# Last expert mixture: expert rows added into a DRAM table by accumulating indirect DMAs, instead of gathered back

## The reference

```python
x = x + _L3_ffn_ref(_layernorm(x, axis=-1), L3_ffn_gate_w, L3_ffn_w1, L3_ffn_w2)

def _L3_ffn_ref(x, gate_w, w1, w2):
    router_logits = jnp.einsum('bsd,de->bse', x, gate_w)
    top_logits, top_idx = jax.lax.top_k(router_logits, TOP_K)
    top_w = jax.nn.softmax(top_logits, axis=-1)
    combine = jnp.sum(jax.nn.one_hot(top_idx, N_EXPERTS, dtype=x.dtype) * top_w[..., None], axis=-2)
    h = jax.nn.silu(jnp.einsum('bsd,edf->ebsf', x, w1))
    y = jnp.einsum('ebsf,efd->ebsd', h, w2)
    out = jnp.einsum('ebsd,bse->bsd', y, combine)
    return out
```

## Time and profile before

| | us |
|---|---|
| median of 3 runs (lowest to highest) | 2155.83 (2154.03 to 2156.53) |
| span of the profiled execution | 2156.2 |
| last sublayer: placement, 1916.25 (the store of `c_rows`) to 1940.24 (first gather) | 24.0 |
| loop, first gather to the end of the last copy to `y` (2105.14 + 0.37) | 165.3 |
| return, from there to the end of the span | 50.7 |

### The profile page before, as it was taken

One profiled execution on the slowest core, in us unless ns is written; L12 is line 12 of the kernel. 1 busy time (PEld: TensorE's weight loads), 2 busy tenths in 40 slices (PEclk: granted clock), 3 DMA queues, 4 the chain that ended last, 5 costly groups with the idle time before them and its releaser, 6 DMA issues. The chain is left out here.

```text
span 2156.2 us, 31922 instructions
## 1 busy us (share of the span) xinstructions
PE 1694.4 (79%) x9560; PEld 1268.2 (59%) x9561; DVE 1111.4 (52%) x2565; ACT 758.4 (35%) x1808; POOL 438.6 (20%) x451
## 2 busy tenths in 40 slices
PE   5965999999999999999997839629824479847990
PEld 4653666666666666666666629528713147636990
DVE  3335555556555655565554650157666856562212
ACT  1211544445444444444443213204426223312330
POOL 1012111111111221222211122241131500007005
PEclk9977999999999999999997559869957589958995
DMA  5001000000001000000000212151000000014114
GB/s 199 0 0 46 1 1 0 0 0 0 0 1 46 1 1 0 0 0 0 0 1 29 88 63 66 56 195 56 3 27 0 0 3 0 0 40 115 34 36 122
DMA packets 30065, 66.49 MB, mean 31 GB/s; under 512 B 6438, under 2 KB 21815, under 8 KB 28460
## 3 DMA queue, kind: packets, MB, share of 16 engines
q1 hardware_dynamic: 23900, 48.99, 6.3%
q0 software_dynamic: 6096, 16.65, 2.9%
HBM read 51.04 MB, written 14.59 MB: 30 GB/s over the span
## 5 line engine op out<-in xcount | busy, mean ns | idle before, releaser
L1052 PE MATMUL banks<-l_ffn_h2T,l_ffn_w 128*128 128x128 f32 (+1 forms) x1536 | 185.0, 279 | 32.2 <-ACT l_ffn_h2T L1166 32.2
L1052 PEld LDWEIGHTS banks<-l_ffn_h2T,l_ffn_w 128*128 128x128 f32 (+1 forms) x1536 | 173.8, 182 | 42.9 <-issue 39.0
L977 PE MATMUL banks<-l_ffn_in_wqkv,l_ffn_hT 128*128 128x512 f32 x384 | 197.2, 611 | 1.9 <-issue 1.1
L1146 ACT ACTIVATE l_ffn_work<-banks,l_ffn_att_bias,l_ffn_att_scale 128x256 f32<-128x256 f32 x256 | 140.6, 568 | 51.8 <-DVE l_ffn_att_bias L1287 51.8
L942 POOL TENSOR_TENSOR l_ffn_rstd<-l_ffn_ve,neg_half 128x1 f32<-128x1 f32 x32 | 17.8, 557 | 658.2 <-DVE l_ffn_ve L1315 658.2
L1015 PEld LDWEIGHTS banks<-l_ffn_vv,l_ffn_pT 128*128 128x128 f32 x1024 | 119.3, 195 | 33.3 <-ACT l_ffn_pT L1155 29.6
L999 PE MATMUL banks<-l_ffn_kT,l_ffn_qT 128*128 128x512 f32 x256 | 132.8, 601 | 0.0
L1015 PE MATMUL banks<-l_ffn_vv,l_ffn_pT 128*128 128x64 f32 x1024 | 122.7, 279 | 8.8 <-DVE l_ffn_pT L1293 5.1
L1286 DVE TENSOR_REDUCE l_ffn_att_top<-banks 128x2 f32<-128x512 f32 x128 | 88.5, 692 | 62.3 <-PE banks L999 62.3
L256 POOL TENSOR_TENSOR rstd<-mean_var,neg_half 128x1 f32 (+1 forms) x80 | 46.0, 576 | 346.9 <-DVE mean_var L249 346.7
L1176 ACT ACTIVATE l_ffn_gate<-banks,l_ffn_layer_cols 128x128 f32<-128x128 f32 x192 | 59.8, 362 | 136.5 <-PE banks L1052 136.5
(11 more groups left out here) (377 smaller groups left out, 3700.8 us busy)
## 6 DMA issues: line engine op xcount, KB each, us to landing
l_ffn_in_w<-in_L_w SPq DMA_DIRECT2D x2, 4096.0 KB, 20.2
l_experts_y_rows<-l_experts_y SPq DMA_DIRECT2D x63, 128.0 KB, 1.7
l_ffn_in_down<-in_L_down SPq DMA_DIRECT2D x1, 4096.0 KB, 13.0
l_experts_c_rows<-l_route_c_all SPq DMA_DIRECT2D x2, 2048.0 KB, 8.5
l_ffn_in_wqkv<-in_L_wqkv SPq DMA_DIRECT2D x1, 3072.0 KB, 12.8
l_ffn_w<-in_L_w SPq DMA_DIRECT2D x2, 1364.0 KB, 7.0
x_res<-in_x SPq DMA_DIRECT2D x4, 512.0 KB, 5.5
l_ffn_rot<-in_rotary SPq DMA_DIRECT2D x2, 1024.0 KB, 4.8
```

The lines of the kernel that those rows point to most:

```text
L977: mm = pe.matmul(ps[:, m.bank + 1 + n, :], hT[:, m.b, m.odd, ch, 1 - ch:P + 1 - ch], wqkv[:, bass.ds(m.layer, 1), ch, n * INNER:(n + 1) * ...
L1052: mm = pe.matmul(ps[0:FW[j], m.bank + j // 2, to:to + P], w1[:, ch, at:at + FW[j]], h2T[:, ch, m.b, :], start=(j % 2, n, ch) == (0, 0, 0), ...
L1146: ex = nc.scalar.activation(work[:, m.b, slot, :], ps[:, m.bank + slot // 2, (slot % 2) * 2 * P:(slot % 2 + 1) * 2 * P], ACT.Exp, bias=bia ...
```

## The change

`l3_ffn` calls a new function, `adding_experts`, in place of `experts`.

- `c_all` gets eight more columns, and `comb` is written into them, so a gathered row (264 wide) brings the token's eight weights with it. The DRAM table `c_rows` gets one more row, of zeros; empty slots take that row.
- `route` gets an SP block that stores `e.x` (2 MB) to the first 2048 rows of a new DRAM table `sums`, which has 128 rows more for empty slots.
- The placement computes, instead of `back` and the weights, which row of `sums` each slot belongs to (`to_row`). Its 32 products have 117 columns instead of 78, and seven small DVE steps follow them instead of two.
- In the loop ACT multiplies the product by the weight while it copies it: it loads the tile's expert number into a register and takes that column of the gathered rows as the scale. It waits for `y_added`, where it waited for SP's store of the same buffer.
- POOL issues 24 gathers, and then for each tile an indirect DMA that adds the 128 rows of `y` to rows of `sums` (line 2241 of the changed kernel). It issues one only when the one before has landed, since two tiles can hold the same token. The other 15 gathers come one behind each of the first 15 adds.
- The return gathers, the weighted sums on DVE and the eight output stores are gone. SP waits for all 39 adds and copies `sums` to the output by one DMA from DRAM to DRAM.

The diff, cut to what the steps above touch:

```diff
-    comb = sb("comb", every)
-    c_all = sb("c_all", [P, ALL_TILES, D])
+    c_all = sb("c_all", [P, ALL_TILES, D + wide])
+    comb = c_all[:, :, D:D + wide] if wide else sb("comb", every)
...
+        if x_to:
+            @block.sync
+            def _(sp):
+                sp.dma_start(x_to[0], e.x[:]).then_inc(x_to[1], 16)
...
+def adding_experts(e, ctx, stage, given, routed, n_tiles, up_weight, down_weight, sums, x_kept):
...
+        @block.gpsimd
+        def _(p):
+            def gather(t):
+                g = 0 if t < until[1] else 1 if t < until[2] else 2
+                p.indirect_dma_start(rows[:, t, :], None, c_rows, bass.IndirectOffsetOnAxis(ap=token[:, t:t + 1], axis=0))\
+                 .then_inc(gathered[g], 16)
+
+            p.wait_ge(c_kept, 32)
+            for t in range(until[2]):
+                gather(t)
+            p.wait_ge(x_kept, 16)
+            for t in range(n_tiles):
+                turn, j = divmod(t, WIDTH)
+                p.wait_ge(s.y_copied.sem, s.y_copied.at(turn, j + 1))
+                if t:
+                    p.wait_ge(added, 16 * t)
+                    p.sem_inc(s.y_added.sem, 1)
+                p.indirect_dma_start(sums, bass.IndirectOffsetOnAxis(ap=to_row[:, t:t + 1], axis=0), y[:, j, :], None, compute_op=ALU.add,
+                                     bounds_check=EMPTY + P - 1, oob_is_err=True).then_inc(added, 16)
+                if until[2] + t < n_tiles:
+                    gather(until[2] + t)
+            p.wait_ge(added, 16 * n_tiles)
+            p.sem_inc(s.y_added.sem, 1)
...
+            def copy_y(m):
+                act_.wait_ge(s.down_psum.sem, s.down_psum.at(m.turn, m.k))
+                act_.wait_ge(s.y_added.sem, s.y_added.at(m.turn, m.k - WIDTH))
+                x = act_.value_load(expert_of[0:1, bass.ds(m.turn * WIDTH + m.j, 1)], min_val=0, max_val=E8 - 1)
+                nc.scalar.activation(y[:, m.j, :], ps[3 + m.j][:, 0:D], ACT.Copy,
+                                     scale=flat(rows[:, bass.ds(m.turn * WIDTH + m.j, 1), bass.ds(x + D, 1)])).then_inc(s.y_copied.sem, 1)
...
+    with nc.Block() as block:
+        @block.sync
+        def _(sp):
+            sp.wait_ge(added, 16 * n_tiles)
+            sp.dma_start(e.out.rearrange("p k d -> (p k) d"), sums[0:EMPTY]).then_inc(e.stored, 16)
+            sp.wait_ge(e.stored, 16)
...
-        routed = route(e, ctx, "l3_route", given, False)
-        experts(e, ctx, "l3_experts", given, routed, KEEPING_TILES, False, lambda x: w1[:, bass.ds(x, 1), :, :].rearrange("p x c n -> p (x c n)"),
-                lambda x, f: w2[:, bass.ds(x, 1), f, :].rearrange("p x n -> p (x n)"), False)
+        x_to = sums[0:ALL_TILES * P].rearrange("(p k) d -> p k d", k=ALL_TILES)
+        routed = route(e, ctx, "l3_route", given, False, EXPERTS, (x_to, x_kept))
+        adding_experts(e, ctx, "l3_experts", given, routed, KEEPING_TILES, lambda x: w1[:, bass.ds(x, 1), :, :].rearrange("p x c n -> p (x c n)"),
+                       lambda x, f: w2[:, bass.ds(x, 1), f, :].rearrange("p x n -> p (x n)"), sums, x_kept)
```

More of the change, by code:

```diff
@@ L143, in __init__ @@
         self.y_copied = new("y_copied")
+        self.y_added = new("y_added")
         self.y_stored0 = new("y_stored0")
@@ L1600, in __init__, with route @@
                                     (self.p_col, "p_col"), (self.tri32, "tri")] + [(w, of) for w, (_, _, of) in zip(self.weights, weights)])
-def route(e, ctx, stage, given, gates_are_softmax):
+def route(e, ctx, stage, given, gates_are_softmax, wide=0, x_to=None):
     nc, s, ps = e.nc, e.s, e.ps
@@ L1665, in keep_c @@
                 k = m.it + m.b * TILES
-                v.tensor_scalar(tile_of(c_all, m.it, m.b), tile_of(e.x, m.it, m.b), flat(e.mean_var[:, bass.ds(k, 1), 0:1]),
+                v.tensor_scalar(tile_of(c_all[:, :, 0:D], m.it, m.b), tile_of(e.x, m.it, m.b), flat(e.mean_var[:, bass.ds(k, 1), 0:1]),
                                 e.rstd[:, bass.ds(k, 1)], ALU.subtract, ALU.mult)
@@ L2882, in l3_ffn @@
     w1, w2 = given.weights
+    sums = e.nc.dram_tensor("l3_sums", (ALL_TILES * P + P, D), F32).ap()
+    x_kept = e.dma_sem("l3_x_kept")
     with ExitStack() as ctx:
-        routed = route(e, ctx, "l3_route", given, False)
-        experts(e, ctx, "l3_experts", given, routed, KEEPING_TILES, False, lambda x: w1[:, bass.ds(x, 1), :, :].rearrange("p x c n -> p (x c n)"),
-                lambda x, f: w2[:, bass.ds(x, 1), f, :].rearrange("p x n -> p (x n)"), False)
+        x_to = sums[0:ALL_TILES * P].rearrange("(p k) d -> p k d", k=ALL_TILES)
+        routed = route(e, ctx, "l3_route", given, False, EXPERTS, (x_to, x_kept))
+        adding_experts(e, ctx, "l3_experts", given, routed, KEEPING_TILES, lambda x: w1[:, bass.ds(x, 1), :, :].rearrange("p x c n -> p (x c n)"),
+                       lambda x, f: w2[:, bass.ds(x, 1), f, :].rearrange("p x n -> p (x n)"), sums, x_kept)
 def rotary():
```

209 lines of the change are left out of this document (added).

## The result

| | us |
|---|---|
| predicted (8 in 10 range) | 2145 (2119 to 2190) |
| changed kernel, median of 4 runs | 2168.42 (2167.3 to 2173.03) |
| kernel before, median of 4 runs beside them | 2155.18 (2154.03 to 2156.53) |
| ratio, 95% interval | 1.0067 [1.0053, 1.0081] |
| span of the changed kernel's profiled execution | 2166.0 |

The change costs 13.2 us where 11 us less were forecast. This is the second rival, adds slower than break-even. A repeat on another chip gave 2166.45 us (9 runs), ratio 1.0041 [1.0027, 1.0055]; there the kernel before against itself came out at 0.9997 [0.9985, 1.0008].

What follows compares the result with a forecast made beforehand. PE was taken to bound the loop, with a 50.7 us return behind it. Terms: -50.7 return, +1.3 placement, +28.5 later end of adds, +9.9 rest: 11 us less than 2156.2, forecast 2145 us, range 2119 to 2190.

Steps and rivals of the forecast that it cites:

- the second rival: Chain of adds in the last loop: adds too slow, period up to 5.3 us, time 2160 to 2190 us; chance 0.33.
- break-even: Chain of adds: at a period of 4.48 us, 3.7 us to land, the span ends at 2156.2 as before.
- What bounds the kernel now: Last sublayer: PE paces the loop at 3.73 us a tile; the return behind it takes 50.7 us, all there is to win.
- Placement: Path to the first gather: wider products and seven small steps instead of two cost +1.3 us (bounds 0 and +2.2).
- ACT's register load: ACT's copy to `y` in the loop: a load of 0.58 us, hidden in 1.33 us free before silu.
- gathers between adds: POOL in the loop: gathers between the first 15 adds, 1.25 us each, fit into POOL's waiting and add nothing.
- clock: PE in the loop: busy 89%, its clock may fall to half, span 2267 us; held unlikely, chance 0.03.
- Value: 2.7 + 0.7 = 3.4, period T = 4.2 us: Each add: a gather's 2.7 us plus 0.7 for twice the bytes read, plus 0.8 wake-up; bounds 3.5 and 5.3.
- The chain as what decides: Loop: each add waits for the last one's landing, so 39 adds at 4.2 us pace it, ending at 2135.35.
- SP wakes 0.8 us later by the same step: End of the kernel: SP issues the output copy 0.8 us after the last add has landed.
- The rule of the Trainium skill: Price of an add: 2.6 us for 256 KB by this rule, so adds would keep up with PE; that rival's chance 0.12.
- The copy from DRAM to DRAM: End of the kernel: the 2 MB output copy takes 8.8 us, as the store of `c_rows` does (bounds 7 and 17.6).

Runs made afterwards that it cites:

- the scatter: The changed kernel with a plain indirect write in place of the accumulate, so table rows are overwritten: 2126.54 us (one run).
- the two tables: The changed kernel with odd tiles added to a second table, two adds in flight, both tables summed at the end: 2128.25 us, ratio 0.986 to the kernel before.
- chip 12: Repeat of the unaltered changed kernel beside the unaltered kernel before on another chip: 2166.45 against 2155.93 us.

## Why the prediction was wrong

- **What bounds the kernel now**: right. The return's 50.7 us went, the adds pace the loop, and 3.73 us for a tile was the right yardstick; the scatter and the two tables ran at 3.67 and 3.62.
- **Placement, ACT's register load, gathers between adds, clock**: right (1.2 us against 1.3; PE's pauses behind ACT 1.0 us at the most, and no loss of pace in the kernels whose adds do not hold ACT up; 1.80 us left over; clock 1.00).
- **"Value: 2.7 + 0.7 = 3.4, period T = 4.2 us"**: this term failed. It measured 3.8 and 4.67. The chain as what decides was right; the price of its link was off, and so was the reason for it. I priced the accumulation as twice the bytes read, +0.7 us over a gather. The plain scatter lands in 2.4, so the accumulation is +1.4, and in the place of more bytes the runs show 0.56 us of longer issue and three times the packets for the same bytes. Two errors partly cancel by luck: the gather's 2.7 was 0.3 above the operation's own base of 2.4, and the extra term 0.7 too small, so the landing is off by only 0.4. 39 x 0.4 of landing and 38 x 0.07 of wake are the 18.3 us. The forecast had named the condition: off by more than 0.3 us, it is wrong. I had also put POOL's longer issue among the reasons of the rival, with no price; it is 0.6 us for each add.
- **"SP wakes 0.8 us later by the same step"**: failed too, by 6.0 us. I took the wake of a store inside a block and overlooked that the copy stands in the next block, behind a barrier that drains POOL. The trace of before held such drains, one behind each of the two mixtures' loops, the second with 21.0 us:

```profile
L1893 POOLq DRAIN  x2: 18261/19636/21011, 1294.8 to 1974.5; - x2
```

  It was hidden because POOL had issued its last gather at 1989.4 and PE ran on until 2105. What ended last before was not POOL, so a drain cost nothing; now POOL ends last.
- **The copy from DRAM to DRAM**: right, 8.7 against 8.8.
- **The rule of the Trainium skill, "DMA: Bandwidth & Descriptors", section "Anatomy of one DMA"** (about 2.0 us fixed plus bytes by 436 GB/s): its estimate of 2.3 us for 128 KB agrees with the plain scatter's 2.4. For the add it gives 2.6 with twice the bytes, and the trace says 3.8; the measurement decides.
- **Break-even** was put at T = 4.48. With the measured tail it is 4.48 - 6.0 / 39 = 4.33; the measured 4.67 lies 0.34 above it, and 0.34 x 39 = 13.3 us agrees with the 13.2 measured. On chip 12, with a period of 4.63, it gives 11.9, and 9.9 were measured.

## What to carry to other kernels

A DMA that must wait for the one before it is priced by its full period, landing plus wake, and is to be held against the tile time of the engine it feeds; where it is longer, split the dependence (two tables) rather than shorten the operation. An accumulating indirect DMA is its own operation: take its time from one that accumulates. When POOL becomes the last engine of a block, its drain at the barrier comes onto the path, so issue the next DMA from inside the block. The other engines' drains at this barrier were short (ACT 0.36 us, DVE 0.55, PEld 1.38).

## What the runs showed of the hardware

- An indirect DMA of 128 rows of 1 KB that accumulates in DRAM: 1.55 us to issue on POOL and 3.8 to land; the same without accumulation 0.99 and 2.4; a gather 0.95 and 2.8 to 3.0 (medians of three lines), 2.6 at the least. With 512-byte rows the period of a chain is 4.27 instead of 4.60 to 4.69 us. Two in flight land in 4.0.
- The accumulating DMA has 144 packets for 0.13 MB, the plain scatter 48 for the same bytes.
- POOL's drain at the end of a block took 6.4 us from the landing of its last indirect DMA.
- A 2 MB copy from DRAM to DRAM landed in 8.2 to 8.8 us; a 2 MB store from SBUF in 6.3 (`x`) and 8.8 (`c_rows`, before).
- On two of the chips ACT and DVE stood still for up to 25 us while POOL issued a long run of gathers. The sign of a change of 0.6% depended on it.
